# The opening of a two-layer transformer kernel in another order: rows normalised ahead of the mask's work, roles copied by four heads, later weights loaded in the second phase

## What is computed

```python
# block 0 (per batch): modulated norm, attention with a bias tensor and a mask
emb = silu(sin_emb(timestep)) @ W_ada + b_ada;  scale, shift = split(emb)
x = ln(src) * (1 + scale) + shift
scores = q k^T / 4 + attention_bias          # bias: 4 x 16 x 512 x 512, 67 MB
probs = softmax(where(src_mask, -inf, scores))
x = x + probs v @ Wo + bo
out0 = x + gelu2(ln(x) * g2 + beta2 @ W1 + b1) @ W2 + b2
# block 1 (per batch): causal attention, no bias tensor
h = ln(out0) * gamma1 + beta1;  x1 = out0 + causal_attention(h) @ Wo + bo
x2 = x1 + gelu(ln(x1) * gamma2 + beta2 @ W1 + b1) @ W2 + b2
out = out0 + gate * (x2 - out0)
```

## Time and profile before

| what | value |
|---|---|
| runs | 942.32 us median of 3 (942.27 to 947.09) |
| the profiled execution | 943.82 us, span 942.1 us, mean granted PE clock 0.944 |
| busy share of the span | PE 86%, DVE 62%, ACT 53%, POOL 46% |
| DMA | 114.75 MB, mean 122 GB/s |
| opening, up to the first addition of scores | 41.54 us |
| X-1, then X0 | up to about 130 us, up to about 256 us |

### The profile page before, as it was taken

The page is one execution under the profiler, slowest core; times in us unless marked ns, Lnnn a source line. Parts: engine busy times, 40 slices in busy tenths (PEclk is TensorE's granted clock), DMA queues, the critical chain, the costliest instruction groups (busy, mean ns, idle before and its releaser), DMA issues.

```text
span 942.1 us, 14630 instructions
## 1 busy us (share of the span) xinstructions
PE 812.1 (86%) x4860; PEld 490.4 (52%) x4860; DVE 580.4 (62%) x1662; ACT 495.7 (53%) x881; POOL 437.3 (46%) x445
## 2 busy tenths in 40 slices
PE   6789878999878987979898889998999898689877
PEld 2455546567433644645645445676646363434545
DVE  6679766756647753778648846767746754636121
ACT  1388866667502345868732466677732426155521
POOL 4789796955101445795502737497201122113220
PEclk8799989999968999979999999999999998888989
DMA  8897985445640117646841046365521126100000
GB/s 238 198 304 219 312 231 156 124 135 159 177 79 2 46 33 167 196 131 167 259 89 46 24 113 175 118 211 190 138 42 46 46 68 157 24 1 2 2 23 23
DMA packets 80046, 114.75 MB, mean 122 GB/s; under 512 B 7691, under 2 KB 43359, under 8 KB 79971
## 3 DMA queue, kind: packets, MB, share of 16 engines
q1 hardware_dynamic: 79971, 113.81, 43.3%
HBM read 86.33 MB, written 2.10 MB: 94 GB/s over the span
## 4 chain that ended last, share of the span: by engine, by line
PE 63%; DVE 16%; ACT 8%; issue 7%; DMA 3%; SPq 1%; POOL 1%; DVEq 0%; ACTq 0%
PE psD L943 12%; PE psD L931 11%; PE psE L965 7%; PE psC L978 6%; PE psD L903 5%; PE psS L957 4%; PE psC L1023 4%; PE psD L919 3%; DVE tiles L1379 3%; PE psD L910 2%; PE psS L993 2%; ACT tiles L694 2%; PE psE L1011 2%; ACT prob L703 2%; PE psD L889 2%
## 5 line engine op out<-in xcount | busy, mean ns | idle before, releaser
L567 POOL TENSOR_TENSOR tiles<-tiles,mask_neg 128x512 f32<-128x512 f32 x256 | 298.6, 1197 | 60.3 <-DMA tiles<-in_fside_Bx16xSxS 54.1
L1379 DVE CUSTOM_DVE_ANT_0 tiles<-psS,tiles 128x512 f32<-128x512 f32 x256 | 173.3, 686 | 119.4 <-PE psS L957 109.2
L703 ACT ACTIVATE prob<-psE 128x512 f32<-128x512 f32 x256 | 151.3, 599 | 78.3 <-PE psE L965 71.1
L694 ACT ACTIVATE tiles<-tiles,rmax 128x512 f32<-128x512 f32 x224 | 162.2, 726 | 42.7 <-DVE rmax L1379 41.9
L965 PE MATMUL psE<-ident,tiles 128*128 128x128 f32 x1024 | 162.5, 282 | 13.2 <-ACT prob L703 12.9
L965 PEld LDWEIGHTS psE<-ident,tiles 128*128 128x128 f32 x1024 | 126.8, 144 | 63.7 <-ACT prob L703 34.5
L613 POOL TENSOR_SCALAR_AFFINE_SELECT prob<-prob 128x256 f32<-128x256 f32 x128 | 51.6, 428 | 192.8 <-ACT prob L715 192.8
L931 PE MATMUL psD<-hT,w 128*128 128x512 f32 x256 | 130.7, 631 | 10.4 <-DVE work L1345 6.8
L1394 DVE CUSTOM_DVE_ANT_0 junk<-psS,later 128x128 bf16<-128x128 f32 x192 | 82.5, 444 | 82.5 <-PE psS L993 81.9
L943 PE MATMUL psD<-w,work 128*128 128x256 f32 x512 | 131.8, 384 | 1.7 <-ACT hT L746 1.7
L957 PE MATMUL psS<-qk 96*128 96x512 bf16 x256 | 101.3, 397 | 24.5 <-DVE rmax L1379 18.3
(11 more groups left out here) (122 smaller groups left out, 1036.1 us busy)
## 6 DMA issues: line engine op xcount, KB each, us to landing
tiles<-in_fside_Bx16xSxS SPq DMA_DIRECT2D x256, 256.0 KB, 3.1
qk<-work SPq DMA_DIRECT2D x96, 256.0 KB, 5.4
w<-in_L_cond_W SPq DMA_DIRECT2D x12, 1024.0 KB, 5.4
res<-in_x SPq DMA_DIRECT2D x4, 512.0 KB, 6.4
out<-x SPq DMA_DIRECT2D x3, 512.0 KB, 2.9
mask_u<-in_mask_Bx1xSxS_bk SPq DMA_DIRECT2D x4, 256.0 KB, 5.2
qk<-mT SPq DMA_DIRECT2D x64, 3.0 KB
prob<-in_L_cond_W_ada SPq DMA_DIRECT2D x1, 512.0 KB
```

Of the source, the lines that this page charges most:

```text
L567: pool.tensor_tensor(tile(b, s), tile(b, s), mask_neg[:, tile_of(s)[1], :], ALU.add).then_inc(masked, 1)
L694: act.activation(tile(b, s), tile(b, s), ACT.Identity, scale=-1.0, bias=rmax[0][:, s:s + 1]).then_inc(shifted_a, 1)
L703: act.activation(prob0[:, part_no % 2, j, :, s % 2 * P:(s % 2 + 1) * P], psE[:, e_no(0, b, s) % 2, :].rearrange("p (k q) -> p k q", k=T), ...
L1379: dve.tensor_tensor_reduce(tile(b, s), psS[:, n % 2, :], tile(b, s), 1.0, -3e38, ALU.add, ALU.max, rmax[0][:, s:s + 1]).then_inc(s_drained, 1)
```

## The change

- The rows of batch 0 are normalised right after the statistics; `measure_mask(0)` comes after the small scalings, `turn_mask(0)` after the first two splits. PE turns the normalised rows ahead of the small vectors, with 2 and 3 idle matmuls more. POOL scales wq, does `inv_std`, waits for the small vectors, then scales wk, fills vx, scales both weights of block 1 (out of X-1), runs the first operation of `modulate(0)`, six masks, and the rest of it. `ada_rows(0)` moves between the q and k projections.
- `modulate(1)` moves from the end of X-1 behind the first six masks of X0.
- `to_roles` copies by groups of four heads: 12 copies of 128 KB, from 64 partitions each, in place of six of 256 KB, with four semaphores. The weights' columns are swapped to match. In the opening, the second half's copies are issued at slot 0 of X-1, after tile 12.
- `w1`, `w2`, x of batches 2 and 3, `wv[1]`, `wo[1]` and the ones table are loaded in X0 at slots 0 to 32.

```diff
+WARM = (2, 0, 3)
-        roles_in = [sem(f"roles_in{c}") for c in range(C)]
+        roles_in = [sem(f"roles_in{g}") for g in range(NG)]
@@ to_roles
-                for r, (i, j) in enumerate(zip(Q_ROLE, K_ROLE)):
-                    pair = part_row[:, c, i:PARTS + j + 1:PARTS + j - i, :]
-                    sp.dma_start(qk6[r:ROWS:ROLES, c * H // C:(c + 1) * H // C, :, :], pair).then_inc(roles_in[c], 16)
+                for g in (2 * c, 2 * c + 1):
+                    if (l, b) == (0, 0) and g == 1:
+                        for n in range(8, RING):
+                            load_tile(n)
+                    rows = slice(g % 2 * P // 2, (g % 2 + 1) * P // 2)
+                    for r, (i, j) in enumerate(zip(Q_ROLE, K_ROLE)):
+                        pair = part_row[rows, c, i:PARTS + j + 1:PARTS + j - i, :]
+                        sp.dma_start(qk6[r:ROWS:ROLES, g * G:(g + 1) * G, :, :], pair).then_inc(roles_in[g], 16)
@@ SP, opening
+            load_raw(1)
+            (bv and bo of block 0) -> rows_first
+            for n in range(4, 8): load_tile(n)
+            to_roles(0, 0, 0)
+            load_x(1)
+            (the other rows, gate) -> rows_in
@@ SP, start() = X-1
+                yield 0
+                to_roles(0, 0, 1)
+                yield 16
                 load_w(0, wo[0], "Wo", wo_in[0])
-                yield 8
-                load_w1(0)
-                yield 12
-                load_w2(0)
...
@@ SP, in_x(0) = X0
+                    yield 0
+                    load_w1(0)
+                    yield 6
+                    load_w2(0)
+                    yield 14
+                    load_x(2)
...
@@ POOL, opening
-            Stream(swap_columns(0)).upto(LAST)
+            first.upto(0)
             inv_std(0, 0, 0)
+            pool.wait_ge(small_ready, N_SMALL)
+            first.upto(LAST)
             for t in (vx[0], vx[1]): memset
+            Stream(swap_columns(1)).upto(LAST)
+            scale_rows(0)
             for s in range(MASK_AHEAD): add_mask(0, s)
-            modulate(0)
+            shift_rows(0)
@@ POOL, X0
+                        pool.wait_ge(rows_in, N_ROWS)
+                        modulate(1)
@@ PE, opening
+            idle(WARM[0])
+            transposed(0, 0, "T1")
...
+            idle(WARM[2])
+            pe.wait_ge(wq_scaled, 1)
             for i in range(2 * C):
                 project_qk(0, 0, i)
+                if i == 1:
+                    ada_rows(0)
@@ DVE, opening
-            mask_known = measure_mask(0)
...
             for half in range(2):
                 normalise(0, 0, 0, res[0], half)
+            (ada4, cols, ada_col, small scalings)
+            mask_known = measure_mask(0)
+            for i in range(2):
+                Stream(split(0, 0, i, 0)).upto(LAST)
             turn_mask(0, mask_known)
-            for i in range(2 * C):
+            for i in range(2, 2 * C):
                 Stream(split(0, 0, i, 0)).upto(LAST)
```

More of the change, by code:

```diff
@@ L633, in projections @@
                 inv_std(l, b, 0)
-                if not l:
-                    yield at.t1 + 2 if at.tail else STEPS - MASK_AHEAD
+                if not l and at.tail:
+                    yield at.t1 + 2
                     modulate(b)
@@ L758, in keep_high @@
                 n = BANK_NO[l, b, "QK", i]
-                act.wait_ge(roles_in[c], N_ROLES * place(l, b))
+                for g in (2 * c, 2 * c + 1):
+                    act.wait_ge(roles_in[g], N_ROLES * place(l, b))
                 wait_bank(act, l, b, "QK", i)
@@ L907, in project_v @@
                 dst = bank(l, b, "V", i)
+                if l and b == 0 and i == 0:
+                    pe.wait_ge(w_in[1], 16)
                 for t in (2 * i, 2 * i + 1):
@@ L983, in scores1 @@
                 n = s_no(1, b, h * T + t)
-                if t == 0 and h % (H // C) == 0:
-                    pe.wait_ge(roles_in[h * C // H], N_ROLES * (place(1, b) + 1))
+                if t == 0 and h % G == 0:
+                    pe.wait_ge(roles_in[h // G], N_ROLES * (place(1, b) + 1))
                 i = h * T + t
@@ L1145, in phase_y, with idle @@
                     the_rest(dense, Y_SLOTS)
+            def idle(n):
+                for _ in range(n):
+                    pe.matmul(psC[:, :], ident_b[:, :], later[:, :], start=True, stop=True)
             pe.wait_ge(made, N_MADE)
-            for _ in range(WARM_UP):
-                pe.matmul(psC[:, :], ident_b[:, :], later[:, :], start=True, stop=True)
+            idle(WARM_UP)
             pe.wait_ge(ada_ready, 1)
@@ L1520, in _ @@
                 normalise(0, 0, 0, res[0], half)
+            dve.wait_ge(ada_in, N_ADA)
+            dve.wait_ge(ada_filled, 1)
+            dve.tensor_tensor(ada4[:, :], psM[0:B, :], bada, ALU.add).then_inc(ada4_ready, 1)
+            dve.wait_ge(ada4_ready, 1)
+            dve.tensor_scalar(ada4[:, 0:D], ada4[:, 0:D], 1.0, None, ALU.add).then_inc(ada4_ready, 1)
+            dve.wait_ge(cols_filled, 1)
+            dve.tensor_copy(cols[:, :], psS[:, 0, 0:N_COLS + N_SWAPPED]).then_inc(cols_ready, 1)
+            dve.wait_ge(ada_turned, 1)
+            dve.tensor_copy(ada_col[:, :, :].rearrange("p i b -> p (i b)"), psS[:, 1, 0:2 * C * B]).then_inc(ada_col_ready, 1)
+            dve.wait_ge(cols_ready, 1)
+            for l in range(2):
+                at = COL_AT[l, "bq"]
+                dve.tensor_scalar(cols[:, at:at + C], cols[:, at:at + C], QSCALE, None, ALU.mult).then_inc(small_ready, 1)
+            at = COL_AT[0, "b1"]
+            dve.tensor_scalar(b1k[:, :], cols[:, at:at + FC], GELU_K / 2, None, ALU.mult).then_inc(small_ready, 1)
+            mask_known = measure_mask(0)
+            dve.wait_ge(small_ready, N_SMALL)
+            for i in range(2):
+                Stream(split(0, 0, i, 0)).upto(LAST)
             turn_mask(0, mask_known)
-            for i in range(2 * C):
+            for i in range(2, 2 * C):
                 Stream(split(0, 0, i, 0)).upto(LAST)
@@ L1528, in _ @@
                 dense = streams(PLANS[kind, b])
+                if (kind, b) == ("X", 0):
+                    dve.wait_ge(rows_in, N_ROWS)
                 if kind == "X":
```

110 lines of the change are left out of this document (49 added, 61 removed).

## The result

The changed kernel takes 942.32 us (median of 20 runs, 936.76 to 947.60), the kernel before, run beside it, 946.78 (20 runs, 942.27 to 951.02). The ratio is 0.9951, 95% interval 0.9933 to 0.9968: 4.5 us faster, just under what was set as a change that can be told (0.5%). The forecast was an effect of -7.15 us and a time of 935.0. Of the 7.3 us by which the time came out higher, 4.5 are the starting level (the three runs shown had a median of 942.3, twenty have 946.8) and 2.7 the smaller effect.

What follows compares the result with a forecast made beforehand. No engine was taken to be at its limit in every stage; the waits that end last bound the kernel. The terms sum to -7.15 us, from 943.8 to 936.7, as a median 935 us, range 930 to 940.

Steps and rivals of the forecast that it cites:

- the opening: Up to the first addition of scores: it comes at about 39.0 in place of 41.54, -2.5 us, bounds -6 to +1.5.
- the start of X-1: Twelve role copies issued between tiles 12 and 13 delay batch 1's normalisation: +2.3 us, bounds 0 to 3.5.
- the rest of X-1: POOL's two scalings leave X-1, so their hold on DVE goes: -0.5 us (0 to -2).
- from X-1 to X0: Mask turning 2.1 us earlier, modulate(1) ahead of mask 6 makes 1.2 late: together -0.9 us, bounds -3 to +2.
- Y0's start, the wait: Half copies end PE's wait for roles at about 257.6, against 260.75: -3.4 us (0 to -4.5).
- Y0's start, the clock: PE may keep the high clock level behind the shorter wait: -2.6 us taken, up to 5.3.
- Y0's end: Six more issues ahead of the last maxima, 4.2 us, and a cold start, 0.8: +5.0 us (+1.5 to +6.5).
- X1 to Y2: Doubled copy issues in Y1 and X1 find room in the queue: 0, up to +1 us.
- Y3's start and the clock: PE's whole wait for roles goes, -2.15 us; the product behind it runs at twice the clock, with neighbours -2.4.
- The first (opening kept): Opening gains -5.0, a half copy costs 0.5 us to issue, X-1's start loses nothing: -15.3 us, 927; chance 0.25.
- The second (clock not recovered): PE enters Y0 and Y3 at the low clock level all the same: sum -2.15 us, 940; chance 0.20.
- The third (half copies land as late as whole ones): Y0 and Y3 start as before and the doubled queue stays: +3.4 us, 946; chance 0.10.

Runs made afterwards that it cites:

- second profile: Each kernel run once more, unchanged: the changed kernel 944.89 us, ratio 0.9967; the kernel before 949.73 us, ratio 1.0021.
- Split start: Changed kernel, with X-1's twelve role copies issued in two lots, behind the tile loads of steps 6 and 12: 937.09 us, ratio 0.9880.
- modulate later: Changed kernel, with modulate(1)'s product behind mask 10 and its sums behind mask 14 of X0: 940.56 us, ratio 0.9921.
- weights back: Changed kernel, with all loads that were moved into X0 issued in X-1 again, as before: 944.39 us, ratio 0.9977.
- Whole copies: Changed kernel, with role copies of eight heads (256 KB) as before, except batch 0's: 949.36 us, ratio 1.0007.

## Why the prediction was right and wrong

The sum beside the ledger, in us:

| step | forecast | measured, first profiles |
|---|---|---|
| the opening, to step 0 | -2.5 | -6.1 |
| the start of X-1, to step 16 | +2.3 | +6.9 |
| the rest of X-1 | -0.5 | +1.0 |
| from X-1 to X0 | -0.9 | +0.3 |
| Y0's start, the wait | -3.4 | -3.2 |
| Y0's start, the clock | -2.6 | -3.5 |
| Y0's end | +5.0 | +2.8 (+0.9 in the second profile) |
| X1 to Y2 | 0 | -0.5 |
| Y3's start and the clock | -4.55 | +0.8 |
| sum | -7.15 | -1.5 |

That the measured effect (-4.5) is within the forecast's range is in part luck: the steps were off by -3.6, +4.6, +5.4 and -2.2 us (the opening, the start of X-1, Y3, Y0's end), which partly cancel. By the two profiles alone the sum, -1.5, would lie outside that range; the medians bring 3 us more that no step explains. The opening and the start of X-1 came out beyond their bounds (-6 to +1.5, 0 to 3.5).

**The start of X-1 is the step that failed most by the experiments.** The mechanism was named (twelve copies between tiles 12 and 13, and POOL waiting), the term was mis-sized: +2.3, bounds 0 to 3.5, measured +6.9 (in the terms of the forecast, by batch 1's normalisation, +5.5: it began at 56.93 with the first addition 6.1 us earlier, 57.54 before). The issue cost was right (0.65 us each, 0.70 forecast). What was wrong is the start: "tile 12's issue" was taken to follow tile 0's turn at S + 2.8 (S is the first addition, 35.44 here), but SP's queue was still behind the second group's copies, batch 1's rows, four bias rows and the gate, and issued tile 12 at S + 5.8. Tile 13 was issued at S + 14.1, not S + 11.7, took 4.0 us to land, not 3.1, and was used at S + 18.1, not S + 14.9. And only batch 1's normalisation was priced, while every addition from step 13 on stood behind the same tile, and the normalisations themselves took longer; PE fell to 1.2 GHz meanwhile. Split start gave back 5.1 us of it in the stage and 0.7 points in the ratio.

**The opening** was mis-sized the other way: -6.1, bounds -6 to +1.5 (4.6 us between the two second profiles). The mask's row was ready, and the first split began, at 20.48 (22.4 forecast), as the chain ahead of it ran earlier (first projection 16.28, forecast 18.2). The two splits took 6.3 us (7.2), of which POOL's hold was 2.5 (0.71 in a subtraction, 1.80 in a cast; 3.3 forecast), and the rest to the first addition 8.65 (9.4). DVE was the late one, as said: the first copies of roles had landed by 32.48. The two terms together were nearly right (-0.2 forecast, +0.8 measured). The reason was the one given, that the start of X-1 eats the opening's gain; the closeness is luck, as both terms were off by some 4 us.

**From X-1 to X0** had both halves right in kind: turning the masks gained 2.0 us (2.1 forecast), and `modulate(1)` cost 2.4 and not 1.2; modulate later takes that away. That X-1 itself loses 1.0 us more (0.9 in the second profile) was not foreseen. In the first profile 0.8 of it comes from step 32 to 42, where two casts take 1.19 and 1.39 us (0.63 and 1.08 before) and a subtraction 1.67 (1.04 before); in the second profile these steps cost nothing. The kernel before loses 0.5 in its own second profile, and weights back loses 0.1. The cause stays open.

**Y0.** The wait fell to 1.47 us (1.3 forecast) and the level stayed high behind it, until 265 (268 in the second profile). Whole copies undid both. At Y0's end the maxima were issued 8.1 us behind the first copy (4.3 before), PE waited 2.23 us for them (0.47 before): 1.8 us and not 4.2, because PE could go on 4.2 us after their issue (352.28 to 356.44), where before it took 5.8 (353.18 to 359.01), behind whole copies the last of which landed only at 358.24; that the landing would get shorter was left out. The cold start behind it came in one profile (4.05 us for the product) and not in the other (2.36).

**Y3 is the other step that failed**: -2.15 for the wait and -2.4 for the clock, measured +0.8. The wait for roles did go (2.15 to none), but PE now waited 1.06 us for ACT at the same place and 0.80 for POOL in front of the product behind it, which so began at 796.68 and not 797.24: what lay behind the wait was not looked up. Where the clock falls in Y2 and Y3 differs between executions of one kernel, so that a gain by the clock there could not be promised; from Y3's first to its last maximum the thirteen profiles take 68.9 to 72.7 us, and the two of the changed kernel 68.9 and 72.7.

**The rivals.** The first (opening kept) was nearer for the opening (-5.0) and wrong for X-1's start and for the 0.5 us of an issue; split start keeps most of the opening's gain through X-1, with 0.9880, 11 to 12 us and not 15.3. The second (clock not recovered) is right for Y3 and wrong for Y0; its sum, -2.15, is about as far from the total as the forecast's. The third (half copies land as late as whole ones) is false: the median is 2.5 us against 5.4 (192 copies, and the 96 of before). 201 GB/s went through in the window above, 212 with whole copies; but 128 KB for each 0.65 us of issuing are 202 GB/s, so the queue set that rate. The Trainium skill's rule that 64 neighbouring partitions reach half of the ports ("SBUF — State Buffer", section "Door 1: The DMA port swizzle") comes with 196 GB/s at 1 MiB; the trace is near that figure and neither shows the limit nor speaks against it.

Still open: what decides where the clock falls in the later stages, whether the moved weights cost or gain a us, the 1.0 us of X-1's middle, and the 3 us between the ledger's sum and the medians.

## What to carry to other kernels

A gain at the start of a pipeline is kept only if the queue that feeds it has the next loads ready: write down, for the first load that is reused, everything that the queue still holds when its slot comes free, and spread a burst of copies among the loads. A wait that goes shows the next one at the same place, so look it up before counting the whole wait. Work of the shared helper engine belongs where its lead over the consumer is large, not in front of the consumer's first steps.

## What the runs showed of the hardware

- The same idle time in front of the same product (2.33 us) left TensorE at 2.4 GHz in one execution of the kernel before and was followed by 1.2 GHz in another (the projection 1.95 or 3.75 us); the changed kernel fell to 1.2 GHz in both and stayed there longer in one (3.50 us or 1.96). One kernel's runs spread over 9 to 11 us.
- A role copy of 128 KB from 64 partitions landed in 2.5 us (median of 192), one of 256 KB from 128 in 5.4 (median of 96), while issuing one took 0.61 us against 0.63 (medians): the queue's time went with the number of copies, the transfer's with the bytes.
- A scaling of 128x4 numbers on DVE took 1.81 us beside POOL's two memsets (17.49 to 19.55) and ended with them, at 19.57. Before, it began during the first of them, took 1.32 and ended with the second (16.65, 16.63); the same scaling takes 0.17 in X-1 (104.39). The hold lasted from one instruction of POOL into the next.
